# Attention loop of a vision block on one NeuronCore: scores ordered by token halves, with narrow passes for the averages and the router

## What is computed

```
h = tokens(x)                                      # three patch levels, Hilbert order, one projection
n = layernorm(h); q, k, v = split(n @ w_inp + b)   # 12 heads of 16
qf, kf = exp(q.omega - diag - max) + eps, ...      # 16 features per head
rhs   = cumsum over tokens of kf (x) v             # causal linear attention
a     = (qf . rhs) / (qf . cumsum(kf) + eps)
h = h + a @ w_out + b_out
n = layernorm(h)
logits = n @ gate_w + gate_b;  v = clip(n @ v_w + v_b)   # the router, 8 + 1 columns
h = h + top-2 of 8 experts(n) + bk_scale * spectrum(v)
```

## Time and profile before

| | us |
|---|---|
| median of 3 runs (lowest, highest) | 883.47 (881.82, 892.5) |
| the profiled execution | 889.71 |
| span of its records | 887.9 |
| PE busy, all of the span | 710.2 (80%) |
| thirteen images of the attention loop, from one qk(0) to the one 13 later (153.9 to 438.6) | 284.7 |

### The profile page before, as it was taken

How to read it: one execution, slowest core, us unless ns; L and a number is a source line. 1 busy time by engine, 2 the same in 40 slices (tenths; PEclk the granted TensorE clock), 3 DMA queues, 4 the chain that set the end, 5 groups by cost and what they waited for, 6 DMA issues and landing times. The chain is left out here.

```text
span 887.9 us, 17124 instructions
## 1 busy us (share of the span) xinstructions
PE 710.2 (80%) x4943; PEld 663.2 (75%) x4944; DVE 512.0 (58%) x1472; ACT 439.4 (49%) x853; POOL 433.9 (49%) x457
## 2 busy tenths in 40 slices
PE   2663279989999999999986049999996999999950
PEld 1353268888888888888886049999996999999950
DVE  1542025756666677676753247888799565656520
ACT  1431045545555555555540137777773666566630
POOL 7761022424444445444432336777774766665443
PEclk9688558968888899898975569999999999999995
DMA  8924100111111111111110023333332334343337
GB/s 213 235 46 157 54 23 14 53 35 44 43 43 43 43 43 52 43 43 43 34 34 22 8 50 54 57 60 58 59 59 43 47 77 71 81 74 78 57 45 142
DMA packets 60016, 55.08 MB, mean 62 GB/s; under 512 B 24232, under 2 KB 51311, under 8 KB 59967
## 3 DMA queue, kind: packets, MB, share of 16 engines
q0 software_dynamic: 19840, 23.53, 15.6%
q1 hardware_dynamic: 35647, 27.76, 11.9%
q10 hardware_dynamic: 4480, 3.21, 1.1%
HBM read 32.52 MB, written 25.10 MB: 65 GB/s over the span
## 5 line engine op out<-in xcount | busy, mean ns | idle before, releaser
L1139 POOL DMA_INDIRECT result<-e_y,e_tag x78 | 138.3, 1773 | 96.9 <-DVE e_y L1469 85.0
L1198 PE MATMUL e_yp<-x_w2s,e_hh 128*128 x468 | 139.4, 365 | 2.0 <-DVE e_y L1469 2.0
L1462 DVE TENSOR_TENSOR e_hl<-e_hid,e_hh 128x512 fp32r<-128x512 f32 x117 | 80.3, 690 | 88.9 <-ACT e_hh L1264 88.6
L502 POOL DMA_INDIRECT tbl_dram<-a_entry,a_slot x64 | 63.1, 986 | 132.1 <-DVE a_entry L985 104.4
L1256 ACT ACTIVATE e_hid<-e_hidden,e_b 128x256 f32<-128x256 f32 x234 | 100.8, 474 | 53.8 <-PE e_hidden L1185 39.2
L1199 PE MATMUL e_yp<-x_w2s,e_hl 128*128 x468 | 117.5, 251 | 0.0
L585 PE MATMUL a_ab<-a_values,a_masked 128*128 (+1 forms) x768 | 113.6, 297 | 0.0
L585 PEld LDWEIGHTS a_ab<-a_values,a_masked 128*128 128x128 f32 x768 | 108.0, 216 | 5.0 <-issue 4.3
L1264 ACT CAST e_hh<-e_hid 128x512 fp32r<-128x512 f32 x117 | 72.4, 621 | 62.0 <-PE e_yp L1199 62.0
L1127 POOL DMA_INDIRECT e_x<-x_dram,e_tag x78 | 80.9, 1037 | 37.8 <-issue 22.9
L1198 PEld LDWEIGHTS e_yp<-x_w2s,e_hh 128*128 128x128 f32 x468 | 87.9, 188 | 2.5 <-issue 2.3
(11 more groups left out here) (252 smaller groups left out, 1623.8 us busy)
## 6 DMA issues: line engine op xcount, KB each, us to landing
a_raw<-in_ew SPq DMA_DIRECT2D x16, 288.0 KB, 2.8
t_hs<-in_ew SPq DMA_DIRECT2D x8, 384.0 KB, 9.3
t_hs<-in_ew SPq DMA_DIRECT2D x16, 192.0 KB, 10.1
h_dram<-t_hs SPq DMA_DIRECT2D x4, 768.0 KB, 4.2
a_hb<-h_dram SPq DMA_DIRECT2D x16, 192.0 KB, 2.4
result<-a_hb SPq DMA_DIRECT2D x16, 192.0 KB, 4.1
x_dram<-a_att SPq DMA_DIRECT2D x16, 192.0 KB, 2.1
spec_dram<-e_space ACTq DMA_DIRECT2D x16, 192.0 KB, 1.9
```

Source lines behind the costliest of these rows:

```text
L1139: pool.indirect_dma_start(out=out, in_=y[:, j], in_offset=None, out_offset=bass.IndirectOffsetOnAxis(ap=tag[:, i % 8, j, 0:1].bitcast(U32) ...
L1198: pe.matmul(Y[:, j, 0:2 * D], hh[:, f, c], w(f, 2 * D), start=f == 0, stop=False, skip_group_check=True)
L1462: g.tensor_tensor(hl[:, f:f + 2].rearrange("p f t -> p (f t)"), hid[:, f:f + 2].rearrange("p f t -> p (f t)"), hh[:, f:f + 2].rearrange("p ...
```

## The change

- `score` and `average` take the steps in the order j, g = n // 3, n % 3 (all three groups of heads of half 0, then of half 1); S and `masked` alternate by n % 2. score(0) waits for the turned keys and queries of half 0 and score(3) for those of half 1. ACT's waits on the scores follow.
- Each pass of an average is 17 columns wide instead of 68, each of the router 9 instead of 45.
- PE: average(0) goes ahead of the prefix counts of `choice`; the queries' features and turn_queries(1) go ahead of the state's passes.
- DVE: the state's instruction goes from the end of round i to behind mask(0) of round i+1 (`take_state`), and mask(1) ahead of `place`.
- POOL: the low part of the weight slice goes ahead of the features' low parts.

```
-GP = 5 * (NE + 1)
+GP = NE + 1
...
@@ -506,22 +505,15 @@
                 if tail:
                     rstd("rstd2_ready", i - 2, mv2, rstd2, "tail", 5 * (i - 2) + 4)
                 if one:
+                    wait_apart(pool, s["high"], i + 1)
+                    v = lambda c: w2s[:, bass.ds(i, 1), :, c * D:(c + 1) * D].rearrange("k u f d -> k (u f) d")
+                    g.tensor_tensor(v(1), raw[:], v(0).bitcast(F32), ALU.subtract).then_inc(s["low"], 1)
                     low_part(i, 0)
                     if not (fixed(i) and i == B - 1):
                         rstd("rstd1_ready", i + 1, mv, rstd1, "norm_step", 5 * (i + 1) + 4)
                     low_part(i, 1)
-                    wait_apart(pool, s["high"], i + 1)
-                    v = lambda c: w2s[:, bass.ds(i, 1), :, c * D:(c + 1) * D].rearrange("k u f d -> k (u f) d")
-                    g.tensor_tensor(v(1), raw[:], v(0).bitcast(F32), ALU.subtract).then_inc(s["low"], 1)
...
@@ -551,14 +543,14 @@
 
                 def score(n):
 
-                    g, j = n // 2, n % 2
-                    if n < 2:
+                    j, g = n // NG, n % NG
+                    if g == 0:
                         pe.wait_ge(s["kT_out"], TJ * b + j + 1)
                         pe.wait_ge(s["qT_out"], TJ * b + j + 1)
                     if not (fixed(i) and i == 1) or n >= 2:
                         pe.wait_ge(s["s_out"], 6 * b + n - 1)
                     for p in range(2):
-                        last = pe.matmul(S[j][:, 2 * p:2 * p + 2].rearrange("p h t -> p (h t)"),
+                        last = pe.matmul(S[n % 2][:, 2 * p:2 * p + 2].rearrange("p h t -> p (h t)"),
                                          kf_t[:, 2 * g + p, j * P:(j + 1) * P],
                                          qb_t[:, 2 * g + p, j].rearrange("p h t -> p (h t)"), start=True, stop=True)
                     last.then_inc(s["s_done"], 1)
@@ -581,9 +573,8 @@
                     pe.wait_ge(s["s_out"], 6 * b + n + 1)
                     for r in range(GH):
                         h = j * H + g * GH + r
-                        own_and_zeros = values[:, (i + 1) % 2, h:TJ * H + 1:TJ * H - h]
-                        last = pe.matmul(beside(o + r * VW), masked[j][:, r],
-                                         own_and_zeros.unsqueeze(1).broadcast_to([P, 2, 2, VW]),
+                        last = pe.matmul(AB[:, o + r * VW:o + (r + 1) * VW], masked[n % 2][:, r],
+                                         values[:, (i + 1) % 2, h],
                                          start=n == 0 and r == 0, stop=True, skip_group_check=True)
                     last.then_inc(s["av_done"], 1)
 
@@ -614,6 +605,8 @@
                     pe.wait_ge(s["att_ready"], i - 1)
                     pe.wait_ge(s["kT_out"], TJ * known(i))
                     turn(R[2], att).then_inc(s["attT_done"], 1)
+                if two:
+                    average(0)
                 if choice:
                     pe.wait_ge(s["chosen_ready"], i - 2)
                     if not fixed(i) or i >= 4:
@@ -625,8 +618,6 @@
                     for j in range(TJ):
                         pe.matmul(all_of, ones[:], count[:, j].unsqueeze(1).broadcast_to([P, TJ, NE]), start=False, stop=False)
                     pe.matmul(M[:, NE:2 * NE], ones[:], chosen[:, 0], start=False, stop=True).then_inc(s["prefix_done"], 1)
-                if two:
-                    average(0)
                 if one:
                     pe.wait_ge(s["xn_ready"], i + 1)
                     if not (fixed(i) and i == 0):
@@ -704,6 +695,13 @@
                 if two:
                     average(5)
                 if one:
+                    pe.wait_ge(s["qT_out"], TJ * i + 1)
+                    for c in range(2):
+                        last = pe.transpose(FA[0:CF, NP * P + c * P:NP * P + (c + 1) * P],
+                                            feat[1][:, c * HC:(c + 1) * HC].rearrange("p h f -> p (h f)"), ident[:])
+                    last.then_inc(s["qf_done"], 1)
+                    turn_queries(1)
+                if one:
                     if not (fixed(i) and i == 0):
                         pe.wait_ge(s["state_out"], i)
                     if tail:
@@ -714,13 +712,6 @@
                                          values[:, i % 2, c * HC:(c + 1) * HC].rearrange("p h v -> p (h v)"),
                                          start=True, stop=True)
                     last.then_inc(s["state_done"], 1)
...
-                    turn_queries(1)
...
@@ -752,14 +743,14 @@
                 def keys_out(j):
                     act.wait_ge(s["kT_done"], TJ * i + j + 1)
                     if two:
-                        act.wait_ge(s["s_done"], 6 * b + 5 + j)
+                        act.wait_ge(s["s_done"], 6 * b + NG * (j + 1))
                     act.copy(kf_t[:, :, j * P:(j + 1) * P], FB[0:CF, 0:NP * P].rearrange("p (n t) -> p n t", n=NP)
                              ).then_inc(s["kT_out"], 1)
 
                 def queries_out(j):
                     act.wait_ge(s["qT_done"], TJ * i + j + 1)
                     if two:
-                        act.wait_ge(s["s_done"], 6 * b + 5 + j)
+                        act.wait_ge(s["s_done"], 6 * b + NG * (j + 1))
                     for r in range(2):
                         last = act.activation(qb_t[:, :, j, r], FA[0:CF, 0:NP * P].rearrange("p (n t) -> p n t", n=NP),
                                               ACT.Copy, scale=own_head[:, r:r + 1])
@@ -869,10 +860,11 @@
                 more = one and not (fixed(i) and i == B - 1)
                 if two:
                     mask(i, 0)
+                    take_state(i - 1)
+                if two:
+                    mask(i, 1)
                 if choice:
                     place(i - 3)
-                if two:
-                    mask(i, 1)
                 if tail:
                     project(i - 2)
                 if one:
@@ -899,13 +891,14 @@
                     apply1(i + 1)
                 if two:
                     normalise(i - 1)
-                if one:
-                    dve.wait_ge(s["state_done"], i + 1)
-                    if two:
-                        dve.wait_ge(s["av_done"], 6 * (i - 1) + 2)
-                    v.tensor_tensor(state[:], M[0:CF, 0:2 * CV].rearrange("p (c x) -> p c x", c=2),
-                                    block_mask[:].rearrange("p h v -> p (h v)").unsqueeze(1).broadcast_to([CF, 2, CV]),
-                                    ALU.mult).then_inc(s["state_out"], 1)
+
+            def take_state(b):
+                dve.wait_ge(s["state_done"], b + 1)
+                if not fixed(b) or b >= 1:
+                    dve.wait_ge(s["av_done"], 6 * (b - 1) + 2)
+                v.tensor_tensor(state[:], M[0:CF, 0:2 * CV].rearrange("p (c x) -> p c x", c=2),
+                                block_mask[:].rearrange("p h v -> p (h v)").unsqueeze(1).broadcast_to([CF, 2, CV]),
+                                ALU.mult).then_inc(s["state_out"], 1)
 
             def normalise(b):
                 ab = AB[:].rearrange("p (j x) -> p j x", j=TJ)[:, :, 0:H * VW].rearrange("p j (h v) -> p j h v", v=VW)

```

More of the change, by code:

```diff
@@ L716, in emit @@
                     last.then_inc(s["state_done"], 1)
[L717 to L723, removed]
             sched(pe, emit)
```

18 lines of the change are left out of this document (4 added, 14 removed).

## The result

The changed kernel takes 956.97 us (median of 4 runs, 954.34 to 959.67) against 887.99 (881.82 to 895.06): ratio 1.080, interval 1.070 to 1.090. The forecast was 966.

What follows compares the result with a forecast made beforehand. The loop was taken as bound by PE's list of work and its clock. Thirteen images going from 21.9 to 27.7 us (+75) plus +8 at the ends gave 973, or 966 us on the median's scale; range 915 to 1010.

Steps and rivals of the forecast that it cites:

- a new hole of over 0.5 us before turn xn2: Sign of being wrong: PE idle over 0.5 us before average(0), turn att or turn xn2.
- Score(1)'s hole goes: PE's 1.71 us idle before score(1), once per image, vanishes because scores 0 and 1 need half 0 only.
- The new wait before average(0): PE waits 0.3 us for mask(0) on DVE, leaving the new order net -1.4 us an image.
- The pace of narrow pairs: PE's load-and-pass pairs stay 0.11 us apart, direct gain 0; far end, not believed, 4.8 us an image.
- What the widths do to the clock: Clock falls in every image's thin part until the dense part; 7.9 us of work at 1.00, image 27.7 us.
- while PE has no hole: Sign of being right: low-clock stretches begin in the averages without PE idle, ending in output projection or qk(0).
- the ends: Second image before the thirteen and last image's thin part and drain behind them: +8 us together.
- POOL and DVE: Slice's 1.41 us moves ahead of low parts; waits before turn xn2 and average(0) +0.2 us, ends 0 and +1.3.
- net -1.4 us an image: New score order: 1.71 us idle goes, 0.3 us wait before average(0) comes; -1.7 to -1.0 as ends.
- Rival A: Clock follows PE's idle time only, so the loop holds 1.00 without the hole: 836 us; chance 0.07.
- B: Clock sees more of each pair than columns; one 6.8 us low stretch an image, about 883 us; chance 0.10.
- C: Dense part reaches 1.00 too late, 7 us at 0.50; image 30.5 us, total 1005; chance 0.20.

Runs made afterwards that it cites:

- narrow_rstd_first: Changed kernel, with the weight slice's low part back behind the features' low parts and rstd2 ahead of POOL's indirect DMAs: 948.6 us, ratio 1.069.
- wide_rstd_first: Changed kernel with old widths (68, 45), the slice's low part back behind the features' and rstd2 ahead of POOL's indirect DMAs: 840.5 us, ratio 0.946.
- old_order_narrow: Kernel before with only the widths changed, averages 17 columns and router 9: 1001.9 us, ratio 1.108.
- order_wide: Changed kernel with the widths of before, averages 68 columns and router 45: 969.1 us, ratio 1.082.
- wf_avg34: wide_rstd_first with averages 34 columns wide, router 45: 889.0 us, ratio 1.001.
- wf_hole: wide_rstd_first with score(1) waiting again for the turned queries of half 1: 859.8 us, ratio 0.968.

## Why the prediction was right, and where it was not

The time, the direction and the place were right, and so was the main reason: the widths alone give 948.6 us (narrow_rstd_first). One part of the reason was wrong, and it did not show in the sum because the two losses don't add. One of the prediction's own signs of being wrong did come: a new hole of over 0.5 us before turn xn2, in eight of the thirteen images.

- *Score(1)'s hole goes*: right. It is gone in every image. The new wait before average(0), forecast 0.3 us, is 0.16 us in most images of the changed kernel and up to 0.6 us where the clock holds (wide_rstd_first).
- *The pace of narrow pairs*: right, 0.97 us for eight loads; the far end of 4.8 us an image did not come.
- *What the widths do to the clock*: right as a mechanism, shown by narrow_rstd_first and old_order_narrow. The clock falls with PE busy throughout (192.32 above), and rises in the dense part in eleven of fourteen cases, in three just ahead of it (308.37 lies right before average(0)). The sign "while PE has no hole" was met in four of the thirteen falls; the other nine come in a wait before turn xn2 or up to 5 us behind one; in narrow_rstd_first every fall is without one. Forecast 27.7 us an image at about 0.63, measured 26.4 at 0.67. A mis-sized term is the work done at 1.00: 7.9 us forecast; the row of the thirteen images gives (2 x 0.67 - 1) x 26.4 = 9.0 us at 1.00 per image. The thirteen images cost +59 instead of +75, the ends +11 instead of +8.
- *POOL and DVE*, the step that failed. It put the extra wait at +0.2 us for the places before turn xn2 and average(0) together, with +1.3 as the far end. Before turn xn2 it measured 12.2 us in thirteen images against 2.0 before, +0.8 an image, with single waits up to 2.7 us. The direction was foreseen (PE earlier against the DMAs). Missed was the second half: the moved slice lands beside norm2 and stretches it from 0.67 to 2.02 us. Missed above all was that a wait of this size costs the clock: I counted its length only. So "net -1.4 us an image" for the new order is refuted. Alone it costs 26.4 - 21.9 = 4.5 us an image (order_wide, on another chip than the 21.9); with POOL's list put right it gains 21.9 - 18.6 = 3.3. One such hole already stood in the trace of the kernel before. The prediction says that all falls in its loop come behind the hole at score(1); nine do, but the low stretch from 182.57 on came behind a hole of 1.18 us before turn xn2, and that image took 29.2 us where the other twelve took 19.8 to 23.1:

```profile
180.42 0.39 PEld L545 LDWEIGHTS a_fb<-ident,a_att 128*96 128x96 f32 x4 [1.18 <-DVE a_att L827]
```

- *Rival A*, idle time only: refuted as a whole by narrow_rstd_first, with next to no idle and 0.66: it took 948.6 us where A has 836. The Trainium skill, "TensorE: Matmul & The Clock Gate", Part 1, has the gate follow how busy PE has recently been. With PE busy 334.11 of 335.37 us by its records and 0.66 granted, this trace does not bear that out for narrow passes. With wide passes and no hole the time that A gave was reached (wide_rstd_first, 840.5).
- *Rivals B and C*: B (no change) is out for 17 columns. wf_avg34 lands near its number, but at another width, and not with B's one low stretch of 6.8 us an image: it has eight of 10.2 to 17.1 us in thirteen images. C's length of 30.5 us came in three images (30.8), each of them with the hole of 2.7 us, which is not C's reason.

What stays open: why the hole at score(1) in the kernel before, 1.71 us in the loads, goes with falls in nine of thirteen images while that of wf_hole, 1.34 us at the same place, goes with none. Their lengths differ, and so does what stands beside them: in wf_hole turn_queries(1) precedes the state's passes and average(0) precedes the prefix counts. No run separates the two. Nor did a run put a hole of one length at both places, so length and place of a hole are not told apart: those of 2.0 and 2.7 us lie between two averages, that of wf_hole ahead of the dense part. What in a narrow pass the clock answers to is not shown either, only that it does. The slice at its new place with rstd2 first was not run alone either.

## What to carry to other kernels

When PE is paced by weight loads, the width of the pass can be free in the pace (here from 17 to 68 columns) and still pay for the clock; look at the granted clock next to the pace before making passes narrow. And when a reordering makes PE earlier, follow the queue of every engine that PE waits for later: here four DMA issues on POOL stood ahead of a 1 us instruction on the critical path, and a reordering that removed a hole of 1.7 us made one of 2.7. A rare long wait in the old trace, with the one long image behind it, is where to look for the price of such a hole. Where two causes each suffice for a loss, taking either one away alone shows next to nothing; only with the other gone did the widths show their 108 us and the hole its 7.8 us an image.

## What the runs showed of the hardware

- Holes are not priced by their length: with wide passes and the new order, a hole of about 2.7 us before turn xn2 goes with 26.4 us an image, one of 2.0 us with 24.3, none with 18.6. The clock in the loop is 0.74, 0.79 and 1.00. A hole of 1.34 us at score(1) cost 0.8 us an image, and the clock stayed at 1.00.
- A PE that is busy 99.6% of 335 us by its records, with 17-column passes behind 128-column fp32 weight loads, is granted 0.66 of full clock (narrow_rstd_first); with 34 columns 0.83 (wf_avg34), with 68 columns 1.00 (wide_rstd_first).
- Two fp32 instructions of 0.37 us each on DVE (0.67 us for both) took 2.02 us together beside one POOL instruction of 1.39 us, and 1.36 us beside POOL's L490.
